# Moving the layer-norm stores from SyncE's queue to ScalarE's in an eight-core attention and FFN kernel

## The reference

```python
x = layernorm(x + attn(x))        # x: (1, 16384, 1024)
#   Q, K, V = x wq', x wk', x wv'    (64 wide)
#   energy  = K' V   (64 x 64, over all tokens)
#   attn    = (Q energy) * sqrt(3/64) wo'
x = layernorm(x + ffn(x))
#   h = silu(x w1' s1) * (x w2' s2)  (4096 wide)
#   h = gelu(h h1' sh1); h = gelu(h h2' sh2)
#   ffn = h w3' s3                   (1024 wide)
```

## Time and profile before

| | us |
|---|---|
| median of the runs | 3298.42 (3296.76 to 3300.09) |
| the profiled execution | 3296.52 |
| its span on the slowest core (core 4) | 3295.0 |
| spans of the 8 cores | 3287.6 to 3295.0 |
| mean granted TensorE clock of the cores | 0.948 to 0.953 |

### The profile page before, as it was taken

How to read it: one execution, slowest core, us unless ns; L and a number is a source line. 1 busy time by engine, 2 the same in 40 slices (tenths; PEclk the granted TensorE clock), 3 DMA queues, 4 the chain that set the end, 5 groups by cost and what they waited for, 6 DMA issues and landing times.

```text
span 3295.0 us, 40257 instructions; the slowest of 8 cores (3287.6 to 3295.0 us)
## 1 busy us (share of the span) xinstructions
PE 2825.1 (86%) x16327; PEld 1438.3 (44%) x16601; DVE 429.4 (13%) x801; ACT 556.1 (17%) x662; POOL 243.6 (7%) x460
## 2 busy tenths in 40 slices
PE   5772688899999999999999559989999999999980
PEld 4661344444444444444444224434444444444440
DVE  1112111111111111111111232210000000000002
ACT  4552333300000000000000133310000000000012
POOL 3320011000000000000000000000000000000000
PEclk9885899999999999999999779999999999999995
DMA  8993455455555555555555323322222122222112
GB/s 121 151 148 96 97 115 107 102 124 129 130 130 130 130 123 129 130 130 130 130 120 129 119 93 105 109 83 77 77 77 75 55 87 77 77 77 77 64 58 96
DMA packets 89170, 347.16 MB, mean 105 GB/s; under 512 B 10904, under 2 KB 10976, under 8 KB 70560
## 3 DMA queue, kind: packets, MB, share of 16 engines
q0 software_dynamic: 64800, 218.73, 34.4%
q10 hardware_dynamic: 14976, 92.28, 6.9%
q1 hardware_dynamic: 9216, 33.56, 2.9%
HBM read 361.83 MB, written 109.05 MB: 143 GB/s over the span
## 4 chain that ended last, share of the span: by engine, by line
PE 76%; DMA 4%; DVE 4%; ACT 3%; issue 3%; DVEq 0%; SPq 0%; ACTq 0%; POOL 0%; POOLq 0%
PE PA L620 30%; PE PB L620 30%; PE PT L584 3%; PE PA L524 3%; PE PB L532 3%; PE PA L532 3%; PE PB L524 3%; DMA X1R<-x 2%; DVE WTB L595 2%; ACT WTB L491 1%; DMA X1R<-x1s 1%; ACT TS L346 1%; DVE X1F L415 1%; DVE X1F L375 1%; DVE X1F L692 1%
## 5 line engine op out<-in xcount | busy, mean ns | idle before, releaser
L620 PE MATMUL PA<-HB,WTB 128*128 128x512 bf16 x2498 | 563.4, 382 | 17.8 <-DMA WTB<-h1t 7.4
L620 PE MATMUL PB<-HB,WTB 128*128 128x512 bf16 x2500 | 557.7, 379 | 3.2
L620 PE MATMUL PA<-GB,WTB 128*128 128x512 bf16 x1999 | 447.9, 380 | 9.7 <-DMA WTB<-h2t 7.2
L620 PE MATMUL PB<-GB,WTB 128*128 128x512 bf16 x1998 | 446.1, 379 | 2.6
L620 PEld LDWEIGHTS PA<-HB,WTB 128*128 128x128 bf16 x2560 | 249.9, 98 | 312.4 <-issue 23.5
L620 PEld LDWEIGHTS PB<-HB,WTB 128*128 128x128 bf16 x2560 | 248.9, 98 | 292.5
L595 DVE COPY WTB<-PT 128x1024 bf16<-128x1024 bf16 x288 | 192.5, 689 | 988.8 <-PE PT L584 988.7
L620 PEld LDWEIGHTS PA<-GB,WTB 128*128 128x128 bf16 x2048 | 199.4, 98 | 242.7 <-issue 9.9
L620 PEld LDWEIGHTS PB<-GB,WTB 128*128 128x128 bf16 x2048 | 198.9, 98 | 234.2
L584 PE MATMUL PT<-IDB,WSB 128*128 128x128 bf16 x2304 | 164.9, 220 | 53.6 <-DVE WTB L595 45.6
L584 PEld LDWEIGHTS PT<-IDB,WSB 128*128 128x128 bf16 x2304 | 142.7, 98 | 98.7 <-issue 65.5
(11 more groups left out here) (116 smaller groups left out, 1374.5 us busy)
## 6 DMA issues: line engine op xcount, KB each, us to landing
WSB<-h POOLq DMA_DIRECT2D x128, 512.0 KB, 7.4
XB<-x POOLq DMA_DIRECT2D x128, 256.0 KB, 6.4
h1t<-WTB ACTq DMA_DIRECT2D x32, 1024.0 KB, 8.2
h2t<-WTB ACTq DMA_DIRECT2D x32, 1024.0 KB, 8.2
WTB<-h1t POOLq DMA_DIRECT2D x32, 1024.0 KB, 5.1
WTB<-h2t POOLq DMA_DIRECT2D x32, 1024.0 KB, 5.1
WSB<-w POOLq DMA_DIRECT2D x64, 256.0 KB, 5.4
wt<-WTB ACTq DMA_DIRECT2D x32, 512.0 KB, 6.0
```

What stands on the lines that cost most here:

```text
L620: first=first, last=last, src_buf=src_buf: fi(t.matmul(PP[rp][:, g_i * 512:(g_i + 1) * 512], WTB[:, so * H + b * 1024 + j * 128: so * H + ...
```

## The change

The stores of both layer norms leave SyncE's list and go to ScalarE's, and SyncE keeps the loads. In `emit_b3` the store of a tile is put behind ScalarE's X1T copy of the same tile, so behind the square root of the next one. In the final layer norm the store of a tile is kept back (`st["pend"]`) and issued at the start of the next step, ahead of the next tile's cast; a ninth call issues the last one. There the first two loads get a wait for landed stores.

```diff
@@ emit_b3
                 lnv = emit_ln(r, r)
-                w('y', 'v', lnv)
-                if tau >= 2:
-                    w('y', f'z{r}', x1st[tau - 2])
-                else:
-                    w('y', f'z{r}', zsnap[r])
-                em('y', lambda s_, th=th, r=r: s_.dma_start(
-                    out=x1s[th * 128:(th + 1) * 128, :],
-                    in_=X1F[:, r * E:(r + 1) * E]).then_inc(SYS[r], 16))
-                x1st[tau] = inc(f'z{r}', 16)
+                lnvs[tau] = lnv
...
                 x1te[tp] = inc('s')
+                w('s', 'v', lnvs[tp])
+                if tp >= 2:
+                    w('s', f'z{rp}', x1st[tp - 2])
+                else:
+                    w('s', f'z{rp}', zsnap[rp])
+                em('s', lambda s, tp=tp, rp=rp, h=h: s.dma_start(
+                    out=x1s[(8 * h + tp) * 128:(8 * h + tp + 1) * 128, :],
+                    in_=X1F[:, rp * E:(rp + 1) * E]).then_inc(SYS[rp], 16))
+                x1st[tp] = inc(f'z{rp}', 16)
@@ make_final_ln, step
+            pt = st["pend"]
+            if pt is not None:
+                pr = pt % 2
+                w('s', 'v', st["lnvs"][pt])
+                if pt >= 2:
+                    w('s', f'z{pr}', outst[pt - 2])
+                else:
+                    w('s', f'z{pr}', zsnap[pr])
+                em('s', lambda s, th2=8 * h + pt, pr=pr: s.dma_start(
+                    out=y[th2 * 128:(th2 + 1) * 128, :],
+                    in_=X1F[:, pr * E:(pr + 1) * E]).then_inc(SYS[pr], 16))
+                outst[pt] = inc(f'z{pr}', 16)
+                st["pend"] = None
+            if tau >= 8:
+                return
...
                 w('y', f'y{r}', ysnap[r])
                 w('y', 'v', vsnap)
+                w('y', f'z{r}', zsnap[r])
...
-            w('y', 'v', lnv)
-            if tau >= 2:
-                w('y', f'z{r}', outst[tau - 2])
-            else:
-                w('y', f'z{r}', zsnap[r])
-            em('y', lambda s_, th=th, r=r: s_.dma_start(
-                out=y[th * 128:(th + 1) * 128, :],
-                in_=X1F[:, r * E:(r + 1) * E]).then_inc(SYS[r], 16))
-            outst[tau] = inc(f'z{r}', 16)
+            st["lnvs"][tau] = lnv
+            st["pend"] = tau
@@ half 1, behind emit_stage1
+            fstep0(8)
@@ last layer norm
-    for tau in range(8):
+    for tau in range(9):
```

More of the change, by code:

```diff
@@ L381, in emit_b3 @@
     def emit_b3(h):
-        attn = {}; addv = {}; x1tp = {}; x1te = {}; xdma = {}; x1st = {}
+        attn = {}; addv = {}; x1tp = {}; x1te = {}; xdma = {}; x1st = {}; lnvs = {}
         ysnap = {0: C['y0'], 1: C['y1']}
@@ L650, in make_final_ln @@
     def make_final_ln(h, two_buf=False):
-        st = {"ftp": {}, "fte": {}, "addv": {}, "xdma": {}, "outst": {}}
+        st = {"ftp": {}, "fte": {}, "addv": {}, "xdma": {}, "outst": {},
+              "lnvs": {}, "pend": None}
         nb = 2 if two_buf else 1
```

## The result

The changed kernel took 3227.6 us (median of 11 runs) against 3301.7 for the kernel before, timed beside it; the ratio is 0.9766, with a 95% interval of 0.9747 to 0.9784. Forecast were 3226 us, and against the 3298.4 known then a ratio of 0.978. Some executions of a kernel fall into a second, slower state of the chip (2 of the 11 here, and 2 of the 4 in experiment 4, which has no ratio for that reason): the medians take them in, the ratios and intervals leave them out. The profiled execution took 3223.3 us, where the sum gave 3224.3; its slowest core is core 4 again, with a span of 3221.8 us against 3295.0.

What follows compares the result with a forecast made beforehand. In three layer-norm stretches loads were held on SyncE behind stores waiting for the normalise. Gains 25.1 + 27.3 + 21.6 = 74.0 us less 1.8 us costs gave 72.2 us, forecast 3226 us, range 3214 to 3245.

Steps and rivals of the forecast that it cites:

- What bounded the tile: In `emit_b3`, each load queued on SyncE behind a store awaiting the normalise, so its 4.3 us lay open every tile.
- Stores in `emit_b3`: Store issued at +3.6 us, landing 2.9 us later, period 6.6 us (upper bound 7.6); gains 25.1 and 27.3 us.
- Rival C: Stores from ScalarE's queue land late, 6.0 us; `emit_b3` period 9.7 us, total 3263 us; chance 0.07, intermediate cases included.
- Rival E: ScalarE stands still until its store has landed; slower from a 3.8 us landing on, 3356 us at 6.0; chance 0.03.
- Last layer norm: The cast comes onto the path behind the waiting store; period 6.95 us, stretch 49.95 us, gain 21.6 us.
- What it costs: Time given back at the stretches' first loads and in stage 1: 0.6 + 0.5 + 0.7 = 1.8 us.
- (a): A stretch's first two loads leave together; in two stretches the first lands perhaps 0.3 us later, 0.6 us in all.
- (b): First final-layer-norm load inside stage 1 waits for the store of tile 6, issued at +6.5 us; costs 0.5 us.
- (c): At seven later stage 1 steps the store's issue may push the cast; 0.1 us each, 0.7 us, at most 3.
- D: Load not freed: another issuing engine saves only the issue, 0.40 us per tile, 8 us; about 3292 us; chance 0.03.
- A: The forecast itself, with store landings of 2.6 to 3.3 us; own range 3215 to 3234 us; chance 0.67.
- B: The DMA issue waits until ScalarE has finished; `emit_b3` period 7.6 us, total 3240 us; chance 0.20.

Runs made afterwards that it cites:

- experiment 4: Changed kernel, but in `emit_b3` the store on ScalarE also waits until the X1T copy has finished; 3238.6 us in the profiled execution, 3242.2 in one other.
- experiment 2: Changed kernel, but in the final layer norm the kept-back store is issued behind the next tile's cast; 3214.2 us, ratio 0.9756 to the kernel before.
- experiment 6: Kernel before with only `emit_b3` changed, the final layer norm keeping its stores on SyncE; 3242.8 us, ratio 0.9833.
- experiment 3: Changed kernel, stores on ScalarE, but each load on SyncE again waits for the normalise of the tile before; 3288.8 us, ratio 0.9981 to the kernel before.
- experiment 1: Kernel before, all stores left on SyncE, each load put one place ahead of the store that held it back; 3204.1 us, ratio 0.9730.

## Why the prediction was right, point by point

*What bounded the tile.* The step "the load stands behind the store on SyncE's queue, and the store waits for the normalise" holds. The run with that wait put back has a ratio of 0.9981 where the change has 0.9766, so it loses 0.0215 of 0.0234 (in the stretches 62 of 76 us) with the stores still on ScalarE, and the run with the load moved ahead on the old queue has shorter stretches than the change.

*Stores in `emit_b3`.* Issue at +3.6 forecast, +3.56 found; period 6.6 forecast, 6.22 to 6.31 found in ten of twelve. The term that was off is the landing: 2.6 us for the 2.9 that I took from a store with a load right behind it. The period's other reading, 7.6 us with a queue that waits for its engine, is what the run with the forced wait gave (7.4). Rival C fell with the landing of 2.6 us. Rival E fell in the last layer norm: there the cast starts at 3183.48, 0.49 us behind the issue of a store, long before that store can have landed (4.9 us at the median of this stretch).
The rule that the prediction cites from the Trainium skill, "PSUM — Partial Sum Buffer", section "Engine vs sequencer instructions", held here for a DMA issue too: it came at 302.44, and the copy in front of it ran from 302.43 to 303.42.

*Last layer norm.* 6.95 us a period forecast, 7.04 found; the way from the normalise to the cast took 0.63 us, not 0.55. That this cost is the cast's place and not the queue's is shown by experiment 2.

*What it costs.* 1.8 us forecast, some 0.3 found in the places that can be read. (a) The two loads that now leave together at 3151.99 have the first add begin 3.37 us later, where the single one of before needed 3207.19 - 3203.65 = 3.54: two together didn't slow the first. In the first half's `emit_b3` it was 5.28 us against 5.05, but the cores lie too far apart for that to say anything (3.8 to 5.6 now, 3.7 to 5.1 before). (b) The first step inside stage 1:

```profile
1879.72 0.33 SPq L700 DMA_DIRECT2D X1R<-x1s  x1
...
1884.23 1.23 DVE L710 SCALAR_TENSOR_TENSOR X1F<-X1R,FT 128x1024 f32<-128x1024 f32 x1 [4.98 <-ACT FT L691]
```

The load leaves 6.42 us behind the last add of `emit_b3`, as reckoned, but the add waited for the cast all the same, 10.93 us behind that add against 11.21 in the earlier trace rows: nothing shows. (c) A later step, as in the earlier trace rows:

```profile
1911.86 0.69 ACT L540 ACTIVATE TS<-PB,SC 128x512 f32<-128x512 f32 x1 [2.77 <-PE PB L533]
1911.99 0.37 ACTq L670 DMA_DIRECT2D y<-X1F  x1
...
1912.51 1.01 ACT L691 CAST FT<-PT 128x1024 f32<-128x1024 bf16 x1
```

The issue at 1911.99 lies under the activation that runs until 1912.55, and the cast starts 0.65 us behind the activation's start, before 0.59. TensorE's stalls at the seven steps sum to 17.9 us, before 17.6; with the cast ahead of the store (experiment 2) they are 17.6 again. The whole way from `emit_b3` to the last layer norm came out 1.1 us longer in the mean of the cores (1281.9 for 1280.8), but it is 1282.0 in experiment 6 as well, where the final layer norm is that of before, so this can't be put down to the change. The gain of the stretches didn't turn up again as time in stage 1.

*The sum.* The gains were under-reckoned by 2.1 and 1.0 us in `emit_b3` and over-reckoned by 0.7 in the last layer norm, and the costs by 1.5: 3.9 us in all. That the profiled execution still came within 1.0 us of the sum is in part luck: on its slowest core the part between the two `emit_b3` stretches happened to take 4.7 us longer than before, against which the first add came 1.8 us earlier. *D.* The Trainium skill, "DMA: Bandwidth & Descriptors", section "Issuing engines are not separate DMA queues", says that issuing from several engines saves only issue time. That was no argument against this change: with the wait kept in front of the loads, another issuer alone left a ratio of 0.998 (experiment 3); the gain came from taking that wait away, and experiment 1 has it without another issuer. The 14 us that experiment 3 keeps in the stretches are more than 21 issues of 0.40 us, though. The chance I gave to faster by over 2%, 0.63, was low mostly because the border of 2% lay between A and B.

## What to carry to other kernels

A DMA queue is a list in order: a load that stands behind a store waits for the data of the store. Look where a load's buffer came free and where it was issued; if the two are far apart, move the load forward in the list before moving anything to another engine. That was the better change here (ratio 0.973 for 0.977, stretches 17 us shorter), since a store put on a computing engine's list brings its own wait there, and what stands behind it pays (the cast, 1.8 us a tile).

## What the runs showed of the hardware

ScalarE's queue issued a DMA 0.01 us after the start of a 0.99 us copy that stood in front of it; with an explicit wait for the copy it came 285.66 - 284.59 = 1.07 us behind that start. Half-megabyte transfers of one core that leave together on two queues land in 4.5 (load) and 4.9 us (store); in `emit_b3` of the changed kernel, where they don't overlap, they take 3.7 and 2.6; in that of the kernel before, on one queue with the load 0.4 us behind the store, 4.3 and 2.9. The second queue doesn't spare them each other.
